# Routing from un-normalised residuals, finishing tiles one at a time: the end of a fused decoder layer

## The reference, cut to what matters

```python
x = layernorm(x + mamba(x))                      # scans; the first 230 us of the kernel
x = layernorm(x + xattn(x, ctx))                 # res2 = x + attention; x2 = layernorm(res2)
x = layernorm(x + ffn(x))
# ffn, T = 1024 tokens, 8 experts, capacity 160:
logits = tokens @ gate_w                         # (T, 8)
probs = softmax(logits); expert = argmax(probs)
mask = one_hot(expert); pos = cumsum(mask, axis=0) - 1        # place of a token in its expert
sec = mask[:, :, None] * one_hot(pos, 160)       # tokens beyond place 160 are dropped
h = relu(einsum(sec, tokens, w1)); y = h @ w2    # per expert, on its (at most) 160 tokens
out = probs * sec * y summed back to the tokens
```

## Time and profile before

| | us |
|---|---|
| median of 3 runs | 370.71 (370.65 to 370.89) |
| the profiled execution's own time | 371.32 |
| its span, first to last instruction | 369.5 |
| PE busy | 310.6 (84%) |
| DVE busy | 289.4 (78%) |
| ACT busy | 247.4 (67%) |
| POOL busy | 204.3 (55%) |

### The profile page before, as it was taken

One profiled execution on the slowest core, in us unless ns is written; L12 is line 12 of the kernel. 1 busy time (PEld: TensorE's weight loads), 2 busy tenths in 40 slices (PEclk: granted clock), 3 DMA queues, 4 the chain that ended last, 5 costly groups with the idle time before them and its releaser, 6 DMA issues.

```text
span 369.5 us, 5605 instructions
## 1 busy us (share of the span) xinstructions
PE 310.6 (84%) x1757; PEld 191.3 (52%) x1757; DVE 289.4 (78%) x475; ACT 247.4 (67%) x452; POOL 204.3 (55%) x142
## 2 busy tenths in 40 slices
PE   6999697999999998999999999888999763089940
PEld 5444494565556544445454547535666552078820
DVE  2869789999999999999999994796899547212532
ACT  3579978999999989999999984746767610022200
POOL 6501468999999988998889850200000023700374
PEclk9999969999999999999999999999999965559985
DMA  6996211223232331333221000000000000240000
GB/s 159 315 260 229 64 58 59 81 92 114 77 121 89 114 115 63 108 116 113 77 97 57 1 0 2 1 2 0 2 2 0 3 0 17 64 108 2 15 29 14
DMA packets 15377, 26.22 MB, mean 71 GB/s; under 512 B 1972, under 2 KB 8909, under 8 KB 15349
## 3 DMA queue, kind: packets, MB, share of 16 engines
q1 hardware_dynamic: 14580, 24.76, 21.4%
q0 software_dynamic: 768, 1.11, 1.0%
HBM read 23.49 MB, written 2.51 MB: 70 GB/s over the span
## 4 chain that ended last, share of the span: by engine, by line
PE 42%; DVE 29%; POOL 10%; issue 10%; ACT 5%; DMA 2%; POOLq 0%; SPq 0%; DVEq 0%; ACTq 0%
DVE arena L1171 21%; PE bank L698 19%; POOL arena L438 5%; PE bank L742 4%; PE bank L923 3%; DVE acc L1181 3%; PE bank L840 3%; PE bank L1042 3%; PE bank L1052 2%; PE bank L764 2%; POOL out L488 2%; PE bank L942 2%; ACT arena L659 2%; POOL dispatched_tokens L469 1%; PE bank L730 1%
## 5 line engine op out<-in xcount | busy, mean ns | idle before, releaser
L438 POOL TENSOR_TENSOR arena<-arena,k_maskT 128x1024 f32<-128x1024 f32 x64 | 150.5, 2377 | 37.7 <-DVE arena L1158 19.7
L1171 DVE TENSOR_TENSOR_SCAN arena<-bank,arena 128x512 f32<-128x512 f32 x128 | 146.0, 1199 | 0.0
L698 PE MATMUL bank<-ident,arena 128*128 128x128 f32 x716 | 106.2, 282 | 30.2 <-DMA arena<-dispatched_tokens 12.7
L698 PEld LDWEIGHTS bank<-ident,arena 128*128 128x128 f32 x716 | 77.8, 141 | 99.3 <-DVE arena L1171 55.7
L840 PE MATMUL bank<-conv_in_T,ident 128*128 128x512 f32 x192 | 92.8, 593 | 0.0
L551 ACT ACTIVATE bank<-delta,a_neg 128x508 f32<-128x508 f32 x128 | 88.3, 692 | 6.6 <-DVE arena L1171 5.8
L595 ACT ACTIVATE conv_in_T<-bank,c_col 128x256 f32<-128x256 f32 x192 | 80.4, 473 | 12.5 <-PE bank L698 11.7
L450 POOL TENSOR_SCALAR rstd<-moments 128x4 f32<-128x4 f32 (+3 forms) x5 | 1.3, 252 | 75.1 <-DVE moments L1223 75.1
L495 ACT ACTIVATE arena<-bank 128x512 f32<-128x512 f32 (+3 forms) x32 | 13.2, 436 | 41.8 <-PE bank L1032 31.8
L840 PEld LDWEIGHTS bank<-conv_in_T,ident 128*128 128x128 f32 x192 | 31.6, 191 | 15.8 <-issue 15.0
L1181 DVE SCALAR_TENSOR_TENSOR acc<-bank,c_col,acc 128x256 f32<-128x256 f32 x64 | 27.3, 467 | 1.8 <-PE bank L698 1.6
(11 more groups left out here) (168 smaller groups left out, 338.1 us busy)
## 6 DMA issues: line engine op xcount, KB each, us to landing
k_maskT<-b_rows SPq DMA_DIRECT2D x32, 512.0 KB, 3.7
w_sb<-in_L_ffn_w SPq DMA_DIRECT2D x1, 2048.0 KB, 11.2
dispatched_tokens<-zeros SPq DMA_DIRECT2D x1, 650.0 KB, 18.8
x_tok<-in_x SPq DMA_DIRECT2D x1, 512.0 KB, 3.9
ctx_tok<-in_ctx SPq DMA_DIRECT2D x1, 512.0 KB, 3.8
out<-uT SPq DMA_DIRECT2D x1, 512.0 KB, 3.9
arena<-dispatched_tokens SPq DMA_DIRECT2D x2, 130.0 KB, 2.2
arena<-dispatched_tokens SPq DMA_DIRECT2D x1, 260.0 KB, 3.5
```

Of the source, the lines that this page charges most:

```text
L438: gp.tensor_tensor(dBx[g % 2][h], du[:, dr, h, :], b_bc[:, g % RING, :], ALU.mult).then_inc(dBx_ok, 1)
L698: return pe.transpose(dst, src, ident[0:src.shape[0], 0:src.shape[0]])
L1171: ve.tensor_tensor_scan(o, a, v, 0.0, ALU.mult, ALU.add).then_inc(scanned, 1)
```

## The change

Five things change, all behind the scans.

1. **Routing from raw residuals.** The argmax over experts doesn't change when a token's logits are scaled by a positive number, and the mean is taken away by a centred gate: `gate_c = (I - 1/D) @ gate`, computed once with one product ("centred") from a matrix that GpSimd makes at the start. TensorE now turns `res2` (`turn_residuals`, names `raw0`, `raw1`), not x2, and the shifted logits are multiplied by rstd only ahead of the softmax.
2. **Groups of four**, `ROUTES = ((0, 4), (4, 8))`. `raw0` stands inside the attention loop at i = 15; mask, places and slots of batches 0 to 3 come ahead of the last two batches' normalisation on VectorE. GpSimd scatters batches 0 and 1, then computes rstd for the second group, then scatters 2 to 7, of which 4 to 7 have semaphores of their own.
3. **Own banks for the last batches**: the `avq`, `oT`, `wo` of batches 6 and 7 no longer share bank 7.
4. **TensorE kept turning**: behind `count_tokens(1)` stand 16 turns, then 16 behind the slots, 11 behind the landing of each of the batches 4 to 7, and 9 more, all into the bank of `av7`.
5. **Roots on ScalarE**: GpSimd's power instructions for the third norm become `Sqrt` with a bias on ScalarE (one table load ahead) and a reciprocal on VectorE, tile by tile (`DONE`: 0, 1, 2, 3, 8, 4, 5, 6, 7, 9). GpSimd has only the indirect DMAs left.

```diff
-    ROUTES = ((0, B - 2), (B - 2, B))
+    ROUTES = ((0, B // 2), (B // 2, B))
...
-        plan += [("x2T0", 0, 2), ("logits0", 2), ("count0", 2), ("x2T1", 3), ("logits1", 0), ("count1", 1), ("xeT0", 0)]
+        plan += [("raw0", 0), ("logits0", 1), (f"oT{B - 3}", 7), (f"pT{2 * B - 1}", 4, 2), (f"av{B - 1}", 6), ("count0", 2)]
+        plan += [(f"avq{B - 2}", 3), (f"avq{B - 1}", 0), (f"wo{B - 3}", 7), (f"oT{B - 2}", 1), (f"oT{B - 1}", 2)]
+        plan += [(f"wo{B - 2}", 3), (f"wo{B - 1}", 4), ("raw1", 5), ("logits1", 1), ("count1", 2), ("xeT0", 0)]
...
-            sp.wait_ge(dispatched, 16 * B)
+            sp.wait_ge(dispatched[0], 16 * HB)
+            for k in range(1, HB + 1):
+                sp.wait_ge(dispatched[k], 16)
...
+            gp.memset(eps[:, :], EPS).then_inc(centre_ok, 1)
+            gp.tensor_scalar(centre[:, :], ident[:, :], -1.0 / D, None, ALU.add).then_inc(centre_ok, 1)
...
-            for g, (first, last) in enumerate(ROUTES):
-                rstd_of(1, g, first, last)
+            rstd_of(1, 0, *ROUTES[0])
...
                 for b in range(first, last):
+                    if b == 2:
+                        rstd_of(1, 1, *ROUTES[1])
+                    gp.wait_ge(x2_ok, b + 1)
                     gp.indirect_dma_start(d_slots, ...
-            rstd_of(2, 0, 0, B)
...
+            for n, j in enumerate(DONE):
+                gp.wait_ge(tile_ok, n + 1)
+                gp.indirect_dma_start(out_rows, bass.IndirectOffsetOnAxis(token_u[:, j:j + 1], 0), y_tile[:, j, :],
+                                      None, bounds_check=T - 1, oob_is_err=False).then_inc(stored, 16)
...
+            sc.preload_act_table(ACT.Sqrt)
+            sc.wait_ge(centre_ok, 1)
+            sc.wait_ge(var_ok, 3 * B)
+            sc.activation(std[:, :], moments[:, :, 1], ACT.Sqrt, bias=eps[:, :]).then_inc(std_ok, 1)
+
+            def root_of_tile(n):
+
+                j = DONE[n]
+                sc.wait_ge(tile_var_ok, n + 1)
+                sc.activation(tile_std[:, j:j + 1], tile_moments[:, j, 1:2], ACT.Sqrt, bias=eps[:, :]).then_inc(tile_std_ok, 1)
...
                 was_read(f"h{e}", sc.activation(
                     hid[e % 2], bank[:, i:i + 2, :].rearrange("p a (c s) -> p (a c) s", c=2)[:, :, 0:CAP], ACT.Relu))
+                for n in range(len(DONE)):
+                    if DONE[n] < E and DONE[n] == e - 2 or DONE[n] >= E and DONE[n - 1] == e - 2:
+                        root_of_tile(n)
...
+            def turn_residuals(g):
+                first, last_b = ROUTES[g]
+                dst = to_fill(pe, f"raw{g}")
+                for b in range(first, last_b):
+                    wait_read(pe, f"wo{b}")
+                    last = turn(dst[:, S * (b - first):S * (b - first) + S], res2[:, b, :])
+                filled(f"raw{g}", last)
...
-                    last = pe.matmul(dst[:, E * (b - first):E * (b - first) + E], x2T[:, S * b:S * b + S], gate[:, :],
+                    last = pe.matmul(dst[:, E * (b - first):E * (b - first) + E], rawT[:, S * b:S * b + S], gate_c[:, :],
...
+            keep_busy(idle_bank, 16)
+            pe.wait_ge(slots_ok, 4)
+            keep_busy(idle_bank, 16)
+            for k in range(1, HB + 1):
+                pe.wait_ge(dispatched[k], 16)
+                keep_busy(idle_bank, 11)
+            keep_busy(idle_bank, 9)
...
+                wait_read(ve, f"logits{g}")
+                ve.wait_ge(rstd_ok, 2 + g + 1)
+                ve.tensor_tensor(shifted, shifted, over_e(rstd[:, bs], many), ALU.mult).then_inc(gate_d, 1)
...
+                if i == 2 * B - 1:
+                    evacuate("raw0", rawT[:, half(0)])
...
+            end_batch(B - 4)
+            normalize(res2, x2, 1, 0, *ROUTES[0], x2_ok)
             choose_expert(0)
+            place_tokens(0)
+            normalize_values(B - 2)
+            normalize_values(B - 1)
+            add_residual(B - 3)
+            end_batch(B - 3)
+            add_residual(B - 2)
+            add_residual(B - 1)
+            end_batch(B - 2)
+            end_batch(B - 1)
+            choose_expert(1)
             normalize(res2, x2, 1, 1, *ROUTES[1], x2_ok)
-            place_tokens(0)
-            choose_expert(1)
             place_tokens(1)
...
+            def store_tile(j):
+
+                ve.wait_ge(tile_std_ok, DONE.index(j) + 1)
+                link(ve.reciprocal(tile_rstd[:, j:j + 1], tile_std[:, j:j + 1]))
+                ve.tensor_scalar(y_tile[:, j, :], res3[:, j, :], tile_moments[:, j, 0:1], tile_rstd[:, j:j + 1],
+                                 ALU.subtract, ALU.mult).then_inc(tile_ok, 1)
```

More of the change, by code:

```diff
@@ new lines, in copy_values, with copy_out @@
+            def copy_values(b):
+                if b >= 2:
+                    to_read(sc, f"avq{b - 2}")
+                evacuate(f"av{b}", avT[b % 2])
+            def copy_out(b):
+                if b >= 2:
+                    to_read(sc, f"wo{b - 2}")
+                evacuate(f"oT{b}", oT[b % 2], lambda ap: ap[:, 0:S])
+            for i in range(2 * B):
+                if i >= 1:
+                    copy_probs(i - 1)
+                wait_read(sc, f"s{i}")
+                sc.activation(prob[i % 3], prob[i % 3], ACT.Exp, scale=SCALE).then_inc(exp_ok, 1)
+                if i % 2 == 1 and i >= 3:
+                    copy_values(i // 2 - 1)
+                if i % 2 == 1 and i >= 5:
+                    copy_out(i // 2 - 2)
@@ L913, in _ @@
                 filled(f"v{g}", last)
+            pe.wait_ge(centre_ok, 2)
+            pe.wait_ge(moe_w_in, 48)
+            filled("centred", pe.matmul(to_fill(pe, "centred")[:, 0:E], centre[:, :], gate[:, :], start=True, stop=True))
             def scores(i):
@@ L964, in project_out @@
                 filled(f"wo{b}", pe.matmul(dst[:, 0:D], oT[b % 2], qkvoT[:, 3, :], start=True, stop=True))
+            def turn_residuals(g):
[5 more added lines that the diff above has]
+                filled(f"raw{g}", last)
             def gate_logits(g):
                 first, last_b = ROUTES[g]
-                pe.wait_ge(x2_ok, last_b)
-                to_fill(pe, f"x2T{g}")
-                flat = bank[:, where[f"x2T{g}"][0]:where[f"x2T{g}"][0] + 2, :].rearrange("p a t -> p (a t)")
+                dst = to_fill(pe, f"logits{g}")
+                wait_read(pe, "centred")
+                wait_read(pe, f"raw{g}")
                 for b in range(first, last_b):
-                    last = turn(flat[:, S * (b - first):S * (b - first) + S], x2[:, b, 0:D])
-                filled(f"x2T{g}", last)
-                pe.wait_ge(moe_w_in, 48)
-                dst = to_fill(pe, f"logits{g}")
-                wait_read(pe, f"x2T{g}")
-                for b in range(first, last_b):
-                    last = pe.matmul(dst[:, E * (b - first):E * (b - first) + E], x2T[:, S * b:S * b + S], gate[:, :],
+                    last = pe.matmul(dst[:, E * (b - first):E * (b - first) + E], rawT[:, S * b:S * b + S], gate_c[:, :],
                                      start=True, stop=True)
@@ L1338, in _ @@
                 moments_of(x2, b)
+            ve.wait_ge(std_ok, 1)
+            link(ve.reciprocal(rstd[:, :], std[:, :]))
             normalize(x2, y_alone, 2, 0, 0, B, alone_ok)
-            order = [j for now in FINISH for j in now]
             def finish_tile(j):
@@ L1375, in _ @@
                         finish_tile(E + (e - 1) // PER_B)
-            for k in range(stores, len(FINISH)):
-                store_tiles(k)
+            store_tile(E - 2)
+            finish_tile(E - 1)
+            finish_tile(ST - 1)
+            store_tile(E - 1)
+            store_tile(ST - 1)
 _INS = ["x", "ctx_1024", "L0_attn_in_proj_w", "L0_attn_conv_w", "L0_attn_conv_bias", "L0_attn_x_proj_w",
```

189 lines of the change are left out of this document (92 added, 97 removed).

## The result

The changed kernel takes 351.98 us (median of 4 runs, 351.23 to 352.57) against 370.80 beside it (370.65 to 371.19): a ratio of 0.9492, 95% interval 0.9472 to 0.9511. The forecast was 353.8. The profiled execution took 351.23 with a span of 349.5; before, 371.32 and 369.5. A run that took over 1.5% longer than the fastest of its kernel is in a slower state of the chip and stands in no median here; there was one, of 362.09, in e7.

The account below looks back on a forecast made before the run. Three limits behind 290 us: the way to the slots, eight POOL scatters, and experts with a low clock and waiting tail. Gains 8.8 + 3.2 + 5.0 - 0.1 = 16.9 gave 353.8 us, range 350.5 to 359.5.

Parts of the forecast that it names:

- three large terms: Gains forecast for the dispatch (8.8 us), the experts (3.2) and the tail behind them (5.0).
- the early end of the dispatch: Dispatch's best case: POOL alone sets the pace, slots as early as 303.4, scatter 4 at 304.4; gain 10.9 us.
- the tail's terms: Behind the last eoT copy: copy 0.33, stores 0.6 each, finishes 1.0 and 2.0, root with hops 0.35; tile 7 ready 5.4 later.
- Dispatch: From 288.52 us to the last scatter: last scatter at 310.3 instead of 319.08, gain 8.8 us.
- The turns: 85 turns behind the last counts: covered by slots, scatters and loads, cost 0, with 1.4 us kept in the range.
- Experts: First 8.7 us of the experts' PE work at the high clock instead of the low: gain 3.2 us, between 0 and 3.9.
- Tail: Last eoT copy to last output DMA: 7.4 us instead of 12.4, gain 5.0, between 3.5 and 5.4.
- Centred gate: The centred product and its copy stand ahead of the first query: 0.1 us loss.
- Early scatters did get ahead: Rival in the dispatch: no scatter ahead of the second slots, gain falls from 8.8 to 3.6, time 359.0; chance 0.10.
- The roots don't pace the experts: Rival in the experts: ScalarE's wait for a variance delays TensorE's copy, each expert loses 0.5, time 357.8; chance 0.10.
- The clock did not stay low: Rival: turns don't lift a fallen clock, end 6.0 us beyond the loads, experts' 3.2 lost, time 363.0; chance 0.05.
- The slower rival: Rival for the 85 turns: each costs its duration, 0.369 us, not its spacing; experts start at 334.4, time 373.1; chance 0.02.

Follow-up runs that it names:

- e7: Changed kernel with values, turned outputs and projections of batches 6 and 7 all in bank 7 again: 356.89 us.
- e2: Kernel before, with only turns added behind the last counts (8, 9 as each of eight scatters landed, 9 more): 367.33 us, ratio 0.9918.
- e9: Changed kernel, nothing altered, in a new set of runs: 352.15 us.
- e5: Changed kernel with each tile's root taken on GpSimd, one by one, in its list between the output DMAs: 358.72 us.
- e6: Changed kernel with roots on ScalarE but in the five groups of before, one root and reciprocal per group: 353.31 us.
- e4: Changed kernel with the first four scatters held back on GpSimd until the second slots, second rstd moved ahead of them: 358.34 us.
- e3: Changed kernel with 29 turns instead of 9 behind the last landing: 353.85 us.

## Why the prediction was right, step by step

The mechanisms were as forecast; the time came out 1.8 us below, and each of the three large terms was a little small. Two of the forecast's sums are 0.1 off: the early end of the dispatch gives a gain of 10.8, not 10.9, and the tail's terms add up to 5.5, not 5.4, so that its gain is 4.9. Neither changes anything.

- **Dispatch, 8.8 said, 9.8 measured** without the 1.21 of the early turns. With these added back to the changed kernel's times, the chain read: `raw0` full 290.1 (290.1 said), first slots 295.8 (296.1), last `add_residual` 298.6 (299.1), logits 300.9 (301.2), second slots 304.6 (305.4), fifth scatter 305.4 (306.4), last 309.2 (310.3). Half of the miss is `choose_expert` and `place_tokens` of the second group, 4.2 said and 3.8 measured; with four batches their instructions are a little shorter than the six-batch rows that I took them from (the first takes 0.19 instead of 0.21), which makes a part of it. The hop from slots to scatter was 0.8 for the fifth scatter, not 1.0, which the earlier trace rows show for a first one; here too the first hop took 1.05.
- **What made the 8.8** was priced only for the early scatters (5.2). Undone one at a time, early scatters cost 5.3, the banks 5.5, raw residuals of the second group 3.4. That is 14.2 for a gain of 9.8, so they don't add; but the banks, to which the forecast gave one sentence and no price, are worth as much as the early scatters (e7).
- **The turns, 0 said, 0 measured**: -0.13 in the link, of which no part is TensorE's own (it idled 0.2 before the expert's turn). The clock fell at 300.8, where "about 301" was said, and rose 3.1 us into the turns, not 5.9; e2 showed 5.9, and e9, the same kernel as the changed one, 5.3, so the 3.1 is one execution's. The Trainium skill says (page "TensorE: Matmul & The Clock Gate", section "Part 4: PE-mode transpose") that transposes don't bring on the full clock. The traces disagree in three places: 50, 32 and 89 transposes of the identity with nothing else on TensorE, and the clock rose in each.
- **Experts, 3.2 said, 3.57 measured.** The two runs of products gave 2.3 (twice 2.50 minus 1.35), not 2.5, but the 2.9 us of PE work around them gave the other 1.27, where I had counted 0.7: nearly the half that was its bound, so that little of it was held back by waits for ScalarE.
- **Tail, 5.0 said, 5.60 measured.** The last expert's tile was ready 4.7 behind the last copy, where 5.4 was said. The hop to and from ScalarE's root showed up once, as 0.36 (0.35 said), the reciprocal of one column took 0.15, where I had taken 0.26 for sixteen, and VectorE's instructions start up to 0.1 before the one ahead has ended, which I had not counted. The mechanism, roots in one queue with output DMAs, is what e5 shows: 4.2, and e6 adds 0.7 for the groups. These two leave 0.7 of the 5.6 to both together.
- **Centred gate, 0.1 loss said:** not seen. The 50 turns start at 46.91 in both, and at 287.32 the changed kernel is 1.20 ahead, the 1.21 of the 50 turns.
- **Rivals.** Early scatters did get ahead (the first at 295.65), and e4 confirms their price. The roots don't pace the experts: 26.24 to 26.27 in all kernels with them and the turns, and 26.27 in e2 without ScalarE's roots. The clock did not stay low. The slower rival needed 0.34 us a turn; e3 gave less than a third of it.

What stays open: whether the 50 turns are shorter on average in the changed kernel, or only in the profiles at hand (7.34 and 7.34, against one of 8.55). That it needs no change at all is shown by the same 50 turns in e6, 8.55 in the changed kernel's code, and in e2, 7.00 in that of the kernel before. Up to 1.2 of the 18.8 hangs on it.

## What to carry to other kernels

Split both traces at the same few landmarks and compare link by link; the sum must give the span, and a link that moved without an edit in it (here the 50 turns) is then seen at once. Price a change of banks by the whole queue of steps that share the bank, and by the clock that the gaps cost, not by one hop. A root or any small step that a critical engine needs belongs on a queue that holds no DMA issues; and filler work must be trimmed anew whenever what it covers moves.
